# One of four score banks copied out by ScalarE and masked by GpSimd, in a retention layer with a mixture of experts

## The reference

```python
h = rms(x, retn_norm_w)
q = h @ q_w; k = h @ k_w * scaling; v = h @ v_w; g = h @ g_w
qr = theta_shift(q, sin, cos)
kr = theta_shift(k, sin, cos)
qk = einsum('bhsd,bhtd->bhst', qr, kr) * mask      # mask: causal, with a decay per head
denom = clip(abs(sum(qk, axis=-1)), 1.0, None)
o = einsum('bhst,bhtd->bhsd', qk / denom, v_h)
o = silu(g) * rms(o)
x = residual + o @ out_w
```

## Time and profile before

| | |
|---|---|
| time, median of 3 runs (lowest, highest) | 738.39 us (736.25, 744.0) |
| the profiled execution: its time | 739.09 us |
| its span, first to last instruction | 737.3 us |
| busy over the span: PE, DVE, ACT, POOL | 76%, 67%, 39%, 47% |
| attention stage | to about 230 us |
| mask on DVE (L542): number, mean | 64, 683 ns |
| mean granted TensorE clock | 0.893 of full |

### The profile page before, as it was taken

One profiled execution on the slowest core, in us unless ns is written; L12 is line 12 of the kernel. 1 busy time (PEld: TensorE's weight loads), 2 busy tenths in 40 slices (PEclk: granted clock), 3 DMA queues, 4 the chain that ended last, 5 costly groups with the idle time before them and its releaser, 6 DMA issues. The chain is left out here.

```text
span 737.3 us, 14872 instructions
## 1 busy us (share of the span) xinstructions
PE 560.7 (76%) x4194; PEld 483.8 (66%) x4195; DVE 492.3 (67%) x1202; ACT 285.3 (39%) x692; POOL 344.7 (47%) x420
## 2 busy tenths in 40 slices
PE   4268898899864998878388989950389999999900
PEld 1146677777753887767266868840289999999900
DVE  0567888889860648474848687540567777777758
ACT  1244445554532644334133434320344444444400
POOL 1026576677653446656610766672024444444410
PEclk9698999999985999999669999985599999999955
DMA  9121212221002755261132366535484444443177
GB/s 303 68 72 37 65 46 72 71 64 43 28 1 82 221 160 175 71 202 43 43 89 82 135 196 201 182 134 172 110 256 132 131 129 130 129 129 115 67 288 307
DMA packets 66122, 91.82 MB, mean 125 GB/s; under 512 B 8544, under 2 KB 56480, under 8 KB 66080
## 3 DMA queue, kind: packets, MB, share of 16 engines
q1 hardware_dynamic: 56144, 69.79, 31.4%
q0 software_dynamic: 6912, 19.01, 7.1%
q10 hardware_dynamic: 3024, 2.50, 1.0%
HBM read 53.23 MB, written 35.95 MB: 121 GB/s over the span
## 5 line engine op out<-in xcount | busy, mean ns | idle before, releaser
L1623 POOL DMA_INDIRECT results<-yb,xe x80 | 77.0, 962 | 109.6 <-DVE yb L1706 106.9
L1280 POOL DMA_INDIRECT dispatched<-rows,slot x64 | 65.2, 1019 | 46.5 <-DVE slot L1372 27.1
L1755 PE MATMUL bank<-wgu_hi,xT_hi 128*128 x160 | 60.1, 375 | 3.2 <-DVE xT_lo L1687 3.2
L1739 PE MATMUL bank<-ident,xe 128*128 128x128 f32 x160 | 32.0, 284 | 37.8 <-DMA xe<-dispatched 37.3
L1700 DVE TENSOR_TENSOR e_hT_lo<-bank,e_hT_hi 128x256 fp32r<-128x256 f32 x80 | 34.0, 425 | 32.2 <-ACT e_hT_hi L1656 32.2
L980 DVE TENSOR_TENSOR a_lo<-act,a_hi 128x512 fp32r<-128x512 f32 x32 | 28.3, 885 | 39.6 <-ACT a_hi L946 39.2
L1755 PE MATMUL bank<-wgu_lo,xT_hi 128*128 x160 | 52.6, 329 | 0.0
L1755 PE MATMUL bank<-wgu_hi,xT_lo 128*128 x160 | 52.5, 328 | 0.0
L435 POOL TENSOR_TENSOR orms<-omse,neghalf 128x16 f32<-128x16 f32 x16 | 46.7, 2921 | 1.7 <-POOL omse L432 0.8
L1739 PEld LDWEIGHTS bank<-ident,xe 128*128 128x128 f32 x160 | 19.9, 145 | 39.9 <-DMA xe<-dispatched 38.1
L542 DVE TENSOR_TENSOR probs<-bank,causal 128x512 f32<-128x512 f32 x64 | 42.1, 683 | 4.8 <-PE bank L677 4.4
(11 more groups left out here) (235 smaller groups left out, 1920.0 us busy)
## 6 DMA issues: line engine op xcount, KB each, us to landing
dispatched<-fill SPq DMA_DIRECT2D x20, 520.0 KB, 6.8
xe<-dispatched SPq DMA_DIRECT2D x80, 130.0 KB, 2.3
trig<-t_trig SPq DMA_DIRECT2D x16, 512.0 KB, 3.5
stage<-expert_gu SPq DMA_DIRECT2D x16, 352.0 KB, 3.5
wgu_hi<-results SPq DMA_DIRECT2D x11, 512.0 KB, 7.9
xt<-L_attn_x SPq DMA_DIRECT2D x32, 128.0 KB, 3.5
wgu_lo<-results SPq DMA_DIRECT2D x5, 512.0 KB, 16.5
x_rows<-h_all SPq DMA_DIRECT2D x16, 128.0 KB, 2.0
```

Source lines behind the costliest of these rows:

```text
L1280: pool.indirect_dma_start(out=dram["dispatched"], out_offset=bass.IndirectOffsetOnAxis(ap=slot[:, k, t:t + 1], axis=0), in_=rows[:, t, :], ...
L1623: pool.indirect_dma_start(out=dram["results"], out_offset=bass.IndirectOffsetOnAxis(ap=xe[:, r, E:E + 1].bitcast(INT), axis=0), in_=yb[:, ...
L1739: tr = nc.tensor.transpose(t_bank[r % 2][:, k * P:k * P + P], xe[:, r, k * P:k * P + P], ident[:, :])
L1755: mm = nc.tensor.matmul(gu_bank[p][:, 0:GU], xT[xn_][:, p, k, :], wgu[wn][:, k, e, :], start=(k == 0 and i == 0), stop=(k == KB - 1 and i ...
```

## The change

One of DVE's four masks goes to two other engines. ScalarE gets a new step `evacuate_scores`, placed between `split_x2T` and `scale_h`: it copies the score bank with index 2 to its fourth of `probs`, unmasked, and signals `raw`. GpSimd gets a new step `mask_raw`, placed between `rms_h` and `rms_o`: it waits for `raw`, multiplies that fourth of `probs` in place by `causal` and signals m2. DVE's call of `mask(t - 1, 2)` is gone.

```diff
+            def evacuate_scores(t, p):
+                act.wait_ge(S["sc_ps"], per(4, t))
+                wait(act, S["o_ps"], per(1, t - 1))
+                nc.scalar.copy(probs[:, 4 * 2:4 * 2 + 4, :], b_s[2][:, :].rearrange("p (h s) -> p h s", s=P)).then_inc(S["raw"], 1)
...
                 if live(4): split_x2T(t - 4, p)
+                if live(1): evacuate_scores(t - 1, q)
                 if live(0): scale_h(t, p)
...
+            def mask_raw(t, p):
+                pool.wait_ge(S["raw"], per(1, t))
+                pool.wait_ge(S["tables"], ALL_TABLES)
+                nc.gpsimd.tensor_tensor(probs[:, 4 * 2:4 * 2 + 4, :], probs[:, 4 * 2:4 * 2 + 4, :],
+                                        causal[:, :].unsqueeze(1).broadcast_to([P, 4, P]), ALU.mult).then_inc(S["m2"], 1)
...
                 if live(0): rms_h(t, p)
+                if live(1): mask_raw(t - 1, q)
                 if live(2): rms_o(t - 2, p)
...
                 if live(4): split_x2T(t - 4, p)
-                if live(1): mask(t - 1, 2)
                 if live(0): rope(t, p)
```

More of the change, by code:

```diff
@@ L222, in setup_and_attention @@
             silu_c mod_ps mod_sb sgn gates prep
-            st6 mv ve rstd h1 h ssq mse rms hr hT_ps hT_hi hT_lo qk_ps vg_ps rope qk v sg qkT_ps qT kT sc_ps m0 m1 m2 m3 inter o_ps st_ps st_new state
+            st6 mv ve rstd h1 h ssq mse rms hr hT_ps hT_hi hT_lo qk_ps vg_ps rope qk v sg qkT_ps qT kT sc_ps m0 m1 m2 m3 raw inter o_ps st_ps st_new state
             oT oTT_ps rabs den den2 osq og oms omse orms y yT_ps yT_hi yT_lo out_ps x2 ssq2 mse2 rms2 x2r x2T_ps x2_hi x2_lo""".split()
```

## The result

| | before | with the change |
|---|---|---|
| time, median | 739.03 us (4 runs, 736.25 to 744.0) | 759.84 us (4 runs, 758.24 to 763.27) |
| ratio, 95% interval | 1 | 1.0296 (1.0257 to 1.0335) |
| period of `rope_add`, R(5) to R(15) | 10.62 us | 11.99 us |
| start of the attention stage's last rms | 227.06 us | 246.75 us |
| profiled execution: time, span | 739.09, 737.3 us | 763.27, 761.5 us |

The change makes the kernel 20.8 us slower by the medians; 759.7 was predicted. In the profiled executions the attention stage is 19.7 us longer. The other 4.5 us between the two spans lie in the later stages, which the change does not touch; the profiled execution of the changed kernel was also the slowest of its four.

A forecast was written before the change was run, and what follows sets the result against it. The prediction took a new loop through GpSimd's queue as the bound, 12.11 us per period against 10.62. First bodies +4.6, ten periods of +1.5 and the last body +1.8 summed to +21.3, giving 759.7 us, range 752 to 768.

The forecast's parts named there:

- What bounds the kernel: Attention bodies: GpSimd's slack behind rms_h is only 0.3 to 0.5 us, though it is idle a third of the time.
- VectorE's mask on the path: Ahead of rope: removing the 0.68 us mask gains nothing; VectorE waits 0.9 for the projection instead.
- The loop through four engines: From one rope_add to the next, through scores, copy, mask and GpSimd's later steps: 11.90 us, 12.11 with the mse meeting.
- The wait ahead of the mask: GpSimd between rms_h and the mask: it waits 0.5 us for ScalarE's copy.
- The copy's delay of hr: ScalarE's queue: hr and the steps to rope come 0.3 us later per body, bounds 0.1 and 0.4.
- rival 2: Only ScalarE's copy shows, GpSimd's mask being nearly hidden: 742 to 746 us, chance 5%.
- L552: VectorE's state product falls from 1.28 to 0.44 us but meets GpSimd's mse, adding 0.21 per period.
- The first bodies: Start of the attention stage: delay grows from 1.4 us at R(2) to 4.6 at R(5).
- The last bodies: Body 16, after R(15): another mask and wait with nothing to absorb them, +1.8 us.
- Rival 1: TensorE's clock drops after longer quiet stretches between attend and scores: 764 to 770 us, chance 15%.
- Rival 3: Kernel gets faster, about 730 us, through VectorE's relief and a shorter state product: chance 2%.
- Rival 4: GpSimd's mask costs less than 1.28, down to 0.68 us: total 750 to 753 us, chance 8%.

The follow-up runs named there:

- e2: Kernel before plus a GpSimd multiplication of the mask's size on an unread tile, without waiting for scores; all four masks stay on VectorE: ratio 1.011.
- e4: Changed kernel with GpSimd's mask cut to one column of each of four heads, leaving part of the computation out: ratio 1.007 to the kernel before.
- e3: Changed kernel with GpSimd's mask moved behind rms_o, after the long power step: 746.98 us.
- e5: Changed kernel with only two of the bank's four heads copied and masked on GpSimd; VectorE masks the other two from PSUM: 747.7 us.
- e12: Changed kernel with rope_add on VectorE and ScalarE's x2r moved behind square_h of the next body: 742.24 us.
- e9: Changed kernel with rope_add moved from GpSimd to VectorE, directly behind rope: 752.7 us.
- e1: Kernel before plus ScalarE's copy of the score bank into an unread tile; all four masks stay on VectorE: ratio 1.004.
- e11: Kernel before with rope_add on VectorE, state product behind modulate, transpose_qk ahead of transpose_y and both split_yT later: ratio 1.040.

## Why the prediction was right, step by step

- **What bounds the kernel: right.** The slack of GpSimd behind rms_h, 0.3 to 0.5, and not its idle third, decided. e2 and e4 show both sides.
- **VectorE's mask on the path: nothing, right.** DVE's idle time ahead of rope is 0.83 (0.9 was forecast), and e4 shows that even a mask of 0.20 elsewhere gains nothing.
- **The loop through four engines: right, its last term in part by luck.** Scores 5.09 (5.10), hand-over 0.12 (0.12), copy 0.59, hand-over 0.07 (0.12), mask 1.27 (1.28). Omse to second rms takes 5.14 in one body and 4.78 in the next, 4.96 in the mean; I had 4.69 plus 0.21, 4.90. Two slips nearly cancelled there: the 4.69 came from the quicker of two alternating bodies (in the other it was 4.92, from 104.31 to 109.23 in the kernel before), and the meeting of 0.21 comes in every second body only. The mean period is 11.99 for 12.11. e3, e5 and e12 show that it is this loop: each shortens or opens it at another place, and the period follows. e9 opened it and left a second link, which I had not seen.
- **The wait ahead of the mask: wrong in size.** 1.11 instead of 0.5, because rms_h is done at R + 4.77 and not at R + 5.39. The sum goes by the copy and not by rms_h, so it did not suffer; the expectation for e3 did.
- **The copy's delay of hr: the mechanism right, the term too large.** 0.11 a period (e1) instead of 0.3; the low bound, where the next activation starts before the copy's end, was the true value. It is off the loop in the changed kernel, so it did not enter the sum of a period, but it set rival 2.
- **L552: right.** 0.44 in the steady bodies, and it meets mse in every second body (0.41). What I did not name is that `centre` is held up in its place, up to 1.56. GpSimd waits 1.11 behind rms_h for the copy in any case, more than the 1.05 by which `centre` is longer, so it should cost nothing; no run takes it away alone.
- **The first bodies: the sum right to a microsecond, the parts not.** R(2) came 3.3 later, not 1.4; R(5) 3.6, not 4.6. The clock in body 2 is what I missed. The windows of TensorE, 1 us each (busy us, granted clock, DMA share, GB/s), of the kernel before:

```profile
57.00:58.00 1.00, 0.64 (x6) 1.00 0.00 0
```

and the same windows of the changed kernel:

```profile
57.00:58.00 1.00, 0.47 (x12) 0.50 0.00 0
...
61.00:62.00 1.00, 1.00 (x4) 0.50 0.00 0
...
70.00:71.00 1.00, 0.79 (x27) 1.00 0.19 39
```

Before, TensorE had the full clock from 57 us on. With the change the lower clock lasted to 62, through the first four of the projection's twelve matmuls. The copy and hr held TensorE's next work back there (it is busy 0.47 of the microsecond from 57), but that this kept the clock low is not shown. e4 has the same copy at the same place and had the full clock from 57 us on. Its window:

```profile
57.00:58.00 1.00, 0.26 (x2) 1.00 0.00 0
```

Its R(2) is 0.8 later than before and its R(5) 0.1 earlier. e2, without any copy, had the lower clock at 57 (0.50) and an R(2) 2.1 later. So how much of the 3.6 us at R(5) is the change's own and how much the clock's stays open. In body 3 it went the other way: the full clock was kept at 70 us where it was lost before. The delay was 3.2 at R(3), 2.6 at R(4) and 3.6 at R(5), where I had let it grow from 1.4 to 4.6. The collision of `rope_add` with the weight splits came as forecast; both stretch. VectorE's splits in the changed kernel at the start of body 4:

```profile
77.95 3.47 DVE L514 SCALAR_TENSOR_TENSOR wf_lo<-h_all,fw,wf_hi 128x1024 fp32r<-128x1024 f32 x2
```

`rope_add` of that body is the one at 78.05 in the lines of GpSimd above, 2.29.

- **The last bodies:** from R(15) to the last rms 24.45 instead of 22.09, +2.4; 1.8 was the forecast.
- **Rival 1, the clock: did not happen** in the steady bodies, where it is 1.00. The quiet stretch between `attend` and the scores grew even more than I said. TensorE's timeline of the changed kernel:

```profile
113.04 1.08 PE L721 MATMUL bank<-probs,vpad 128*32 128x128 f32 x32
...
118.45 0.50 PE L689 MATMUL bank<-qT,kT_even 32*128 32x128 f32 x8 [0.73 <-ACT qT L343]
```

From 114.12 to 118.45 are 4.3 us, and the clock holds. But the length of the stretch alone does not decide, and the rival went by that length. In body 3 it is 4.6 in both kernels; before, the clock fell behind it, and with the change it stayed at 1.00 (the row for 70:71 above):

```profile
64.55 1.08 PE L721 MATMUL bank<-probs,vpad 128*32 128x128 f32 x32
...
70.21 0.50 PE L689 MATMUL bank<-qT,kT_even 32*128 32x128 f32 x8 [1.17 <-ACT qT L343]
```

In e11 it fell behind a stretch of 4.65. In e9 it fell in one of the steady bodies, behind a stretch of 3.9 like those of its neighbours, and that period was 12.72 where the others are 11.1 to 11.7:

```profile
187.00:188.00 1.00, 1.00 (x17) 0.50 0.00 0
```

So the case was closer than my 15% says; how close, no run here shows.
- **Rival 2 (only the copy shows)** needs GpSimd's work off the loop. e12 is this case, made by hand: 742.2, inside the 742 to 746 that I gave it. **Rival 3 (faster)** is refuted by e4: the loop with a free mask was put at 10.62, with a mask of 0.20 it measured 10.80. **Rival 4 (a cheaper mask):** it measured 1.27.

The sum: +3.6 to R(5), +13.7 for the ten periods, +2.4 behind: 19.7 us in the profiled executions, where 21.3 was forecast, and 20.8 by the medians. The mean period was put 0.12 too high, the first bodies 1 us too high, the last bodies 0.6 too low, and the medians lie 1 us over the attention stage's own loss; the median of the kernel before, too, was 738.4 at the forecast and 739.0 beside the change. The mechanism was right, but that 759.7 and 759.84 lie 0.1 us apart is luck.

## What to carry to other kernels

When work goes to an engine that is idle a third of the time, look at where in its body the idle time lies. Here 1.28 us of work was put behind a wait for data of the same body and ahead of the step that releases the next one, and cost more than its own length, 1.37 us a period. Before moving work, write down for each engine what its queue does after the new step and who waits for that; where the new step can't be earlier, move the urgent steps ahead of it or the new one behind the long step. The same reading found a gain without moving any work: an instruction held up by another engine's use of SBUF, moved by a few places, gave 0.8%.

## What the runs showed of the hardware

- A VectorE instruction with two SBUF operands that runs beside GpSimd's `rope_add`, which reads SBUF, stretches to just past its end: the state product from 0.44 to 1.28, `centre` from 0.51 to 1.56. It goes the other way round too: the two weight splits and `rope_add` took 3.47 and 2.29 beside each other and 2.47 and 1.28 apart, and mse took 0.41 and not 0.19 beside the state product. I had expected it of all these but `centre`. The Trainium skill (SBUF — State Buffer, "Who interferes with whom") says that such a pair contends, and the runs agree; VectorE's masks, with one operand in PSUM, kept their 1.29 for two beside GpSimd's mask (107.64 to 108.93 against 108.30 to 109.57).
- Two activations in a row start 0.48 us apart where the first lasts 0.59 (e1). In a sum over a queue the spacing is the price, and the duration is what a reader on another engine waits for.
